# A graph attention layer on one core: f1's matmuls made 128 columns wide, x's sum moved to TensorE, the size test moved into later gaps, the last store split over two queues

## What is computed

```
x [4096, 128] f32, adj [4096, 4096] int32, W [128, 128], w1, w2 [1, 128], b1, b2 [1]
in_fts = W @ x.T
f1 = (w1 @ in_fts).T + b1          # one number per row
f2 = (w2 @ in_fts).T + b2          # one number per column
logits = f1 + f2.T
coefs = softmax(leaky_relu(logits) + where(adj > 0, 0, -1e9), axis=-1)
out = layernorm(x + coefs @ x, axis=-1)
```

## Time and profile before

| | |
|---|---|
| median of three runs | 273.05 us (272.51 to 273.35) |
| the profiled execution | 272.69 us, of which the profile's span is 270.8 us |
| busy in the span | PE 258.9, PEld 227.4, DVE 244.2, ACT 193.2, POOL 61.3 us |
| granted TensorE clock, mean | 0.994 |
| DMA | 73.64 MB, 272 GB/s over the span |

### The profile page before, as it was taken

How to read it: one execution, slowest core, us unless ns; L and a number is a source line. 1 busy time by engine, 2 the same in 40 slices (tenths; PEclk the granted TensorE clock), 3 DMA queues, 4 the chain that set the end, 5 groups by cost and what they waited for, 6 DMA issues and landing times.

```text
span 270.8 us, 5889 instructions
## 1 busy us (share of the span) xinstructions
PE 258.9 (96%) x2195; PEld 227.4 (84%) x2195; DVE 244.2 (90%) x310; ACT 193.2 (71%) x292; POOL 61.3 (23%) x87
## 2 busy tenths in 40 slices
PE   3989999999999999999999999999999999999990
PEld 3988988888888888888888888888888888888880
DVE  3899999999978999999999499999999999999963
ACT  2599899899999958992899329991999097104140
POOL 4022155000000051005940060006400600054150
PEclk9999999999999999999999999999999999999997
DMA  6999999999999999999999999999999999702011
GB/s 201 263 307 310 310 309 310 290 300 319 315 317 320 313 320 319 319 319 324 313 283 322 348 310 310 312 313 312 306 371 333 329 257 318 190 0 74 4 45 36
DMA packets 22258, 73.64 MB, mean 272 GB/s; under 512 B 2786, under 2 KB 3940, under 8 KB 22244
## 3 DMA queue, kind: packets, MB, share of 16 engines
q1 hardware_dynamic: 11104, 35.20, 43.0%
q10 hardware_dynamic: 9860, 34.61, 42.2%
q0 software_dynamic: 1280, 3.67, 4.6%
HBM read 71.37 MB, written 2.10 MB: 271 GB/s over the span
## 4 chain that ended last, share of the span: by engine, by line
DVE 48%; DMA 15%; PE 15%; issue 8%; ACT 7%; POOL 5%; ACTq 1%; DVEq 1%; POOLq 0%
DVE mn L737 16%; DVE msk L750 9%; DVE mn L742 9%; DMA nat<-in_adj 8%; PE ps L1094 8%; DMA out<-ybt 6%; ACT sgn L470 4%; PE ps L1051 3%; DVE post L858 3%; DVE ybt L873 3%; DVE bns L878 2%; PE ps L1038 2%; POOL xn L369 2%; DVE post L860 2%; DVE ntot L863 2%
## 5 line engine op out<-in xcount | busy, mean ns | idle before, releaser
L1094 PE MATMUL ps<-bt,msk 128*128 128x258 f16 x2048 | 230.3, 274 | 0.0
L1094 PEld LDWEIGHTS ps<-bt,msk 128*128 128x128 fp8e5 x2048 | 200.4, 98 | 29.4
L470 ACT ACTIVATE sgn<-f2b,nf1l 128x1024 int8<-128x1024 f32 x128 | 136.6, 1144 | 2.4 <-issue 1.6
L737 DVE TENSOR_SCALAR mn<-nat 128x4096 int8<-128x4096 int32 x32 | 73.2, 2287 | 3.0 <-DMA nat<-in_adj 2.7
L409 POOL TENSOR_SCALAR nmr<-mv 128x4 f32<-128x4 f32 x7 | 12.9, 1837 | 165.4 <-DVE mv L882 165.4
L615 ACT ACTIVATE ybt<-ybt,nmr,rstd 128x128 f32<-128x128 f32 x28 | 11.5, 483 | 44.1 <-POOL nmr L414 44.1
L750 DVE STREAM_TRANSPOSE msk<-mn 128x1024 uint32<-128x1024 uint32 x32 | 39.8, 1245 | 2.6
L742 DVE SCALAR_TENSOR_TENSOR mn<-sgn,mn 128x1024 uint32<-128x1024 uint32 x32 | 39.2, 1225 | 1.1
L608 ACT ACTIVATE post<-ps,ac 128x258 f32<-128x258 f32 x60 | 24.9, 468 | 10.3 <-PE ps L1094 10.3
L755 DVE TENSOR_SCALAR msk<-msk 128x1024 uint32<-128x1024 uint32 x32 | 22.2, 694 | 1.0
L1051 PEld LDWEIGHTS ps<-vsb,xn 128*128 128x128 f32 x64 | 14.2, 330 | 1.9 <-ACT xn L478 1.8
(11 more groups left out here) (112 smaller groups left out, 104.7 us busy)
## 6 DMA issues: line engine op xcount, KB each, us to landing
nat<-in_adj SPq DMA_DIRECT2D x64, 512.0 KB, 15.4
nat<-in_adj ACTq DMA_DIRECT2D x64, 512.0 KB, 18.5
xn<-in_x POOLq DMA_DIRECT2D x8, 256.0 KB, 12.1
out<-ybt POOLq DMA_DIRECT2D x12, 128.0 KB, 7.5
msk<-in_x SPq DMA_DIRECT2D x8, 128.0 KB, 4.1
msk<-in_x ACTq DMA_DIRECT2D x8, 128.0 KB, 4.4
out<-ybt SPq DMA_DIRECT2D x4, 64.0 KB
out<-post SPq DMA_DIRECT2D x4, 64.0 KB
```

Of the source, the lines that this page charges most:

```text
L470: ins = act.activation(sgn[:, c, g * JA:(g + 1) * JA], f2b[:, :], ACT.Sign, bias=nf1l[:, bass.ds(G * t + g, 1)], scale=-1.0)
L737: dve.tensor_scalar(mn[:, c % 2], nat[:, c], 0, EDGE, ALU.is_gt, ALU.mult).then_inc(cast_done, 1)
L1094: ins = pe.matmul(ps[:, 2 * c + m, 0:2 * DV], mask_f[c][m][:, n // KB, n % KB, :], btv[m][:, n, :], start=(n == first), stop=(n == last - 1))
```

## The change

1. f1_columns for groups 1 to 7 multiplies with the vector repeated 128 times, so each matmul streams 128 columns and writes 128 columns of ps, of which the next matmuls overwrite all but the first. Group 0 keeps its two columns (f1 and f2), with f2's now at column 300.
2. x's column sums are made on PE: 32 float32 matmuls with ones as weights (sum_x), in eight groups of four among the transposes and f1's. The accumulated sums in xT_out, their reduction on DVE and the matmul over xt1 go. xeps_out moves behind signs(2, 2) on ACT.
3. gram moves behind tile 0's minus matmuls, its last part behind tile 1's. The size test's steps move: gram's maximum behind turn(2, 2), stat_max(1, 2, 4) and stat_out(1, 2, 4) among the plus and low_x steps behind it; on PE turn_stats(1, 2, 4) into the middle of tile 2's minus matmuls and widen_stats(1, 2, 4) behind the first plus_sums of tiles 0 and 1.
4. Half of scale_x(0, 3) goes to ACT as scale_last, and the scale_x steps stand behind plus(2, 2).
5. POOL issues load_rows(1), the load of xn's second half, behind rows(0, 0) and no longer behind the next rows.
6. The last tile is stored in four pieces, two from SP and two from ACT, counted by end_stored, on which SP waits behind the end of the branch. SP's waits for the other stores move ahead of the wait for the last tile.

```
@@ block.sync, fast path
+                sp.wait_ge(out_stored, 16 * G * (NQ // 2 - 1))
+                sp.wait_ge(last_stored, 16 * (G + QT - 1))
                 sp.wait_ge(tile_ready, 1)
-                sp.dma_start(out_t[NT - 1], post[:, 1, 0, QT - 1, 0:D]).then_inc(last_stored, 16)
-                sp.wait_ge(out_stored, 16 * G * (NQ // 2 - 1))
-                sp.wait_ge(last_stored, 16 * (G + QT))
+                for g in range(G // 2):
+                    store_end(sp, g)
...
-            sp.nop()
+            sp.wait_ge(end_stored, 16 * G)
@@ block.gpsimd, fast path
                 rows(0, 0)
+                load_rows(1)
                 for turn in range(1, NQ // 2):
                     rows(2 * turn - 1, 1)
-                    if turn == 1:
-                        load_rows(1)
@@ block.scalar
-                act.activation(xT[:, b * 512:(b + 1) * 512], ps[:, 4 + b % 2, :], ACT.Copy,
-                               accum_out=xt8[:, b:b + 1]).then_inc(xT_ready, 1)
+                act.activation(xT[:, b * 512:(b + 1) * 512], ps[:, 4 + b % 2, :], ACT.Copy).then_inc(xT_ready, 1)
...
+            def scale_last():
+
+                act.wait_ge(cs_ready[0], 1)
+                act.wait_ge(table_ready[1], BCH)
+                for i in range(KB):
+                    n = (BCH - 1) * CN + i
+                    ins = act.activation(ybuf[:, BCH - 1, i], xl_chunk(BCH - 1)[:, i], ACT.Copy, scale=cs[:, 0, n:n + 1])
+                ins.then_inc(y3_act, 1)
...
             signs(2, 2)
+            xeps_out()
...
             load_far(QT + 2, 2)
+            scale_last()
             signs(3, 3, between={1: lambda: split_x(0, 2), 2: lambda: split_x(0, 3)})
...
                 normalise_last(1, 2, 1)
+                act.wait_ge(tile_ready, 1)
+                for g in range(G // 2, G):
+                    store_end(act, g)
@@ block.vector
             spread_f1(1, FIRST * KB, NK, 7, 0)
-            dve.wait_ge(xT_ready, NB)
-            dve.tensor_reduce(xt1[:, :], xt8[:, :], AX_X, ALU.add).then_inc(xt1_ready, 1)
...
-            dve.wait_ge(gram_made, 1)
-            dve.tensor_reduce(stat[:, 3:4], ps[:, 4, 0:D], AX_X, ALU.max).then_inc(stat_ready, 1)
             turn(1, 1)
 
             dve.wait_ge(cs_ready[0], 1)
             scale_x(0, 1)
-            stat_max(1, 2, 4)
             cast(2, 2, 0)
-            stat_out(1, 2, 4)
             combine(2, 2)
             dve.wait_ge(y_ready[0], 1)
             turn(2, 2)
+            dve.wait_ge(gram_made, 1)
+            dve.tensor_reduce(stat[:, 3:4], ps[:, 4, 0:D], AX_X, ALU.max).then_inc(stat_ready, 1)
 
             plus(0, 0)
             low_x(0, 1)
             plus(1, 1)
-            scale_x(0, 2)
+            stat_max(1, 2, 4)
             low_x(0, 0)
-            scale_x(0, 3)
+            stat_out(1, 2, 4)
             dve.wait_ge(y_act, 1)
             plus(2, 2)
+            scale_x(0, 2)
+
+            scale_x(0, 3, KB)
             low_x(0, 2)
             low_x(0, 3)
@@ block.tensor
-                        to, v = ps[:, bank, n - n0:n - n0 + 1], vsb[:, D:D + 1]
+
+                        to, v = ps[:, bank, n - n0:n - n0 + P], vsb[:, D:D + 1].to_broadcast([P, P])
...
+            def sum_x(b):
+
+                for n in range(b * KB, (b + 1) * KB):
+                    ins = pe.matmul(ps[:, 2, 0:D], ones[:, :], xl[:, n * D:(n + 1) * D], start=(n == 0), stop=(n == NK - 1))
+                if b == NB - 1:
+                    ins.then_inc(xsum_made, 1)
...
             turn_x(1)
+            sum_x(0)
...
+            sum_x(1)
             f1_columns(2)
             turn_x(4)
             turn_stats(0, 0, 2)
+            sum_x(2)
             f1_columns(3)
             turn_x(5)
+            sum_x(3)
             widen_stats(0, 0, 2)
             f1_columns(4)
             turn_x(6)
+            sum_x(4)
             f1_columns(5)
             turn_x(7)
+            sum_x(5)
+            sum_x(6)
             f1_columns(6)
+            sum_x(7)
             f1_columns(7)
...
-            gram(0)
-            gram(1)
+            pe.wait_ge(turn_done, 1)
+            pe.wait_ge(den_ready[1], 1)
+            minus_sums(0, 0)
+            minus_sums(0, 1)
...
+            minus_sums(0, 2)
+            minus_sums(0, 3)
+
+            pe.wait_ge(xT_ready, NB)
+            gram(0)
+            gram(1)
+            gram(2)
 
             pe.wait_ge(gst_ready, 1)
             pe.wait_ge(turn_done, 2)
             edge_sums(1, 1)
...
+            gram(3).then_inc(gram_made, 1)
             pe.wait_ge(turn_done, 3)
-            edge_sums(2, 1)
+            edge_sums(2, 1, 0, NK // 2)
+            turn_stats(1, 2, 4)
+            edge_sums(2, 1, NK // 2, NK)
...
             plus_sums(ORDER[0], range(2))
+            widen_stats(1, 2, 4)
             plus_sums(ORDER[1], range(2))
+
+            pe.wait_ge(stat_ready, 2)
```

More of the change, by code:

```diff
@@ L131, in gat_kernel @@
         ac = sb("ac", [P, 2, NT], F32)
-        xt8 = sb("xt8", [P, NB], F32)
-        xt1 = sb("xt1", [P, 1], F32)
         xeps = sb("xeps", [P, DV], F32)
@@ L155, in gat_kernel @@
         ORDER = (1, 0, 2, 3)
+        F2_AT = 300
         w_in = sem("w_in")
@@ L203, in gat_kernel @@
         y1_act = sem("y1_act")
+        y3_act = sem("y3_act")
         y_ready = [sem(f"y_ready{m}") for m in range(2)]
@@ L206, in gat_kernel @@
         table_ready = [sem(f"table_ready{m}") for m in range(2)]
-        xt1_ready = sem("xt1_ready")
         xsum_made = sem("xsum_made")
@@ L236, in gat_kernel @@
         out_stored = sem("out_stored")
+        end_stored = sem("end_stored")
         flag_ready = sem("flag_ready")
@@ L279, in load_part, with store_end @@
             eng.dma_start(dst, adj_v[t, a]).then_inc(nat_in[c], 16)
+        def store_end(eng, g):
+            eng.dma_start(out_t[NT - 1, g], post[g * SQ:(g + 1) * SQ, 1, 0, QT - 1, 0:D]).then_inc(end_stored, 16)
         @block.sync
@@ L335, in _ @@
                         apart(sp)
-            sp.nop()
+                sp.sem_inc(end_stored, 16 * G)
+            sp.wait_ge(end_stored, 16 * G)
         @block.gpsimd
@@ L477, in xT_out @@
                 act.wait_ge(x_turned, b + 1)
-                act.activation(xT[:, b * 512:(b + 1) * 512], ps[:, 4 + b % 2, :], ACT.Copy,
-                               accum_out=xt8[:, b:b + 1]).then_inc(xT_ready, 1)
+                act.activation(xT[:, b * 512:(b + 1) * 512], ps[:, 4 + b % 2, :], ACT.Copy).then_inc(xT_ready, 1)
             def f2_copy():
                 act.wait_ge(f1_made, 1)
-                act.activation(f2l[:, 0:KB], ps[:, 0, FIRST * KB:FIRST * KB + KB], ACT.Copy).then_inc(f2l_act, 1)
+                act.activation(f2l[:, 0:KB], ps[:, 0, F2_AT:F2_AT + KB], ACT.Copy).then_inc(f2l_act, 1)
             def f2_sums(i, n0):
@@ L525, in rows_out, with xeps_out @@
                 act.activation(nf1l[:, FIRST * KB:], ps[:, 6, 128 + FIRST * KB:256], ACT.Copy).then_inc(nf1l_ready, 1)
+            def xeps_out():
                 act.wait_ge(xsum_made, 1)
-                act.activation(xeps[:, 0:D], ps[:, 0, 0:D], ACT.Copy, scale=LOW * TINY / N).then_inc(xeps_ready, 1)
+                act.activation(xeps[:, 0:D], ps[:, 2, 0:D], ACT.Copy, scale=LOW * TINY / N).then_inc(xeps_ready, 1)
+            def scale_last():
[5 more added lines that the diff above has]
+                ins.then_inc(y3_act, 1)
             def split_x(m, h):
@@ L537, in split_x @@
                     act.wait_ge(y_ready[0], h)
+                    if h == BCH - 1:
+                        act.wait_ge(y3_act, 1)
                 act.activation(btv[m][:, h * CN:(h + 1) * CN, 0:D], ybuf[:, h], ACT.Copy,
@@ L1047, in f1_columns @@
                     if b == 0:
-                        to, v = ps[:, 0, n:n + FIRST * KB + 1:FIRST * KB], vsb[:, D:D + 2]
+                        to, v = ps[:, 0, n:n + F2_AT + 1:F2_AT], vsb[:, D:D + 2]
                     else:
-                        to, v = ps[:, bank, n - n0:n - n0 + 1], vsb[:, D:D + 1]
+                        to, v = ps[:, bank, n - n0:n - n0 + P], vsb[:, D:D + 1].to_broadcast([P, P])
                     ins = pe.matmul(to, xT[:, n * P:(n + 1) * P], v, start=True, stop=True)
@@ L1123, in _ @@
                       stop=True).then_inc(nf1_made, 1)
[L1124 to L1134, removed]
             minus_sums(0, 2)
             minus_sums(0, 3)
-            widen_stats(1, 2, 4)
+            pe.wait_ge(xT_ready, NB)
+            gram(0)
+            gram(1)
+            gram(2)
             pe.wait_ge(gst_ready, 1)
@@ L1141, in _ @@
             edge_sums(1, 1)
-            pe.wait_ge(xT_ready, NB)
+            gram(3).then_inc(gram_made, 1)
             pe.wait_ge(turn_done, 3)
-            edge_sums(2, 1)
+            edge_sums(2, 1, 0, NK // 2)
+            turn_stats(1, 2, 4)
+            edge_sums(2, 1, NK // 2, NK)
             pe.wait_ge(den_ready[0], 1)
```

## The result

The changed kernel takes 275.1 us, the median of nine runs (273.73 to 275.6), against 272.67 us for nine of the kernel before on the same chip (272.07 to 273.35). The ratio is 1.0074, 95% interval 1.0048 to 1.0101: slower by some 2.0 us by the ratio and 2.4 between the medians, where 3.9 were forecast. The profiled execution took 275.1 us with a span of 273.4, which is 2.4 and 2.6 us more than the one before.

What follows compares the result with a forecast made beforehand. PE's matmul stream was taken as the bound: tile 3 starting 3.8 us later plus 0.1 of tail, +3.9 on the profiled 272.69 us, made 276.6, 277.0 by the median; stated 276.9, range 273.4 to 283.0.

Steps and rivals of the forecast that it cites:

- The bound: PE's stream of 2048 matmuls at 0.1124 us each, never idle from 33.85 us, sets the time.
- The size test: Behind turn(2): copy to gst waits 1.8 us for PE, cast(3) follows after 12.1 us, not 8.6; alone +1.0 us.
- I take 18 us: PE's start: moment when TensorE's clock rises to 2.4 GHz, with bounds of 11 and 35 us.
- The forecast for a float32 matmul: sum_x on PE: 0.48 us per 128-column matmul at 1.2 GHz; four take 1.9 us, or 0.95 at 2.4 GHz.
- the two stalls: DVE waits for PE at its first spread_f1, 1.1 us, and at the first copy to gst, starting at 23.1 us.
- the list of signs: Closing list of what profiles would show, including DVE idle 1.1 us at first spread_f1 and 1.4 at first gst copy.
- early clock: Rival: clock up by about 14 us, first gst copy waits little, size test stays; 274.0 to 275.8 us, chance 0.18.
- the 2.8 us that I had put down to PE: DVE's delay at the first copy to gst, which starts at 23.1 us because it waits for PE's results.
- The lead that I named: DVE's lead over PE at tile 3, 1.6 us, as the most that anything done ahead of it can bring.
- The tail: Last tile's stores and final wait: bounds -0.7 and +0.5 us, taken as +0.1.
- Edits costed at nothing: Dropped accumulated sums on ACT, scale_last, moved xeps_out and the earlier load of xn's second half: no effect on time.
- The rule on transposes: Transposes don't count as busy for the clock, so it rises late; late-clock rival: 278 to 282 us, chance 0.24.

Runs made afterwards that it cites:

- e3: Kernel before with only f1's matmuls of groups 1 to 7 widened to 128 columns; 272.62 us, ratio 1.0005.
- e1: Changed kernel with only DVE's order behind turn(2, 2) altered: scale_x(0, 2) ahead of stat_max, half of scale_x(0, 3) and plus(2, 2) ahead of stat_out; 272.78 us, ratio 0.9986.
- e7: Kernel before with only the moved gram, the moved size test and scale_last; 276.3 us, ratio 1.0118.
- e8: Changed kernel with gram, the size test's steps, scale_x(0, 3) and xeps_out moved back to where they were; 272.27 us, ratio 0.9987.
- e6: Changed kernel with sum_x(0) moved from behind turn_x(1) to ahead of sum_x(1); 274.49 us, ratio 1.0066.
- e5: Kernel before with only the load of xn's second half, load_rows(1), moved forward; 273.56 us, ratio 1.0008.
- e9: Kernel before with e1's order, the new tail and the earlier rows, but narrow f1 and no sum_x; 272.82 us, ratio 1.0001.
- e2: Changed kernel with f1's matmuls back at one column, sum_x kept; 279.29 us, ratio 1.0143.
- e10: e1 with one more wait on SP: first adjacency loads issued only once x's third chunk has landed; 273.34 us, ratio 1.0013.

## Why the prediction was right in direction and twice too large

**The bound held.** The stream runs at 0.112 us a matmul in every kernel, and each profiled span but e3's follows from the start of minus(3) and the tail, within 0.2 us. The changed kernel: +3.2 - 0.6 = +2.6 us of span.

**The size test held, step by step.** Forecast: a wait of 1.8 us at the copy to gst, cast(3) 12.1 us behind turn(2), some 3 us of idle ACT, PE idle ahead of minus(3). Measured: 1.97, 12.3, 3.86, and waits of 0.79 and 1.46. e1, e7 and e8 show that this is the cause, and that nothing else in the change costs what the runs can tell.

**The step that failed is "I take 18 us".** The clock rose at about 10 us in the changed kernel (f1's 16 records take 2.05 us, were 3.58) and at 13 to 14 in e1, e3 and e6. The forecast for a float32 matmul was right at the low level (0.46 us against 0.48, in sum_x(0): 1.84 us from 7.57 to 9.41, four matmuls). So was 0.95 for four at the high level (0.89 between starts, 17.61 to 18.50), though the rows that I took "about half" from, 422 and 273 ns, say 0.65. So what was wrong was the level, and with it the two stalls. The first copy to gst starts at 21.90 without a wait, where I had 23.1 after one of 1.7 (23.1 - 21.4; the 1.4 in the list of signs doesn't fit these steps). f1_made is there at 11.9 us, so the wait of 1.1 at the first spread_f1 isn't there either. turn(2) ends at 42.3 instead of 43.4. This is the rival "early clock", whose 274.0 to 275.8 us hold the result; I gave it 0.18.

Yet turn(2) is 0.8 us later than before: DVE reached spread_f1 at 13.96 instead of 12.38, and made good 0.8 by the work that it lost (0.9 forecast). That delay is no stall on PE: DVE waits 0.86 and 0.88 us for x's chunks. I don't count it to the change. e5, whose start is untouched, shows the same waits (1.34 and 0.68 us), e8, with the changed start, has no late one. It varies between executions. So none of the 2.8 us that I had put down to PE was there in this execution, and x, late in it by chance, put DVE back by 1.6 us at spread_f1 and so filled part of the gap. That the number came as near as it did is luck to that extent.

**The lead that I named was not the tightest.** I took 1.6 us at tile 3 as the limit of any gain. At tile 2 it is 42.2 - 41.5 = 0.7 us, from the same rows. It explains why 1.9 us of earlier start (e3) and 2.4 (e8, 31.47 against 33.85) come out as 0.2 and 0.5: PE then waits for DVE at turn(2).

**The tail** is the second term that was mis-sized: +0.1 forecast, -0.6 measured, near the bound of -0.7. The +0.1 was picked between the bounds without a working; the four issues overlap on two queues (0.89 and 0.80 us, starting 0.06 apart). **Edits costed at nothing**: the moved load was worth nothing that is resolved (e5), and the wait at ybt for the store went, as said; scale_last and xeps_out had no run of their own.

**The sum with the measured terms**: the start of minus(2) +0.1, where 43.4 against 42.2 had been +1.2; from minus(2) to minus(3) +3.1, where it had been +2.6; the tail -0.6 instead of +0.1. Together that is +2.6 us of span instead of +3.9: 1.1 less from the clock, 0.7 less from the tail, 0.5 more behind turn(2).

**The rule on transposes.** From 5 us on, PE had transposes and narrow matmuls alone until 29.4 us in the kernel before and until about 30 in e7 and e9, and no rise before; in the changed kernel, e1, e2, e3, e6, e8 and e10 a group of ordinary 128-column matmuls stands ahead of every rise. That agrees with the Trainium skill, "TensorE: Matmul & The Clock Gate", Part 4, by which transpose mode does not count as busy in the same way. What I had drawn from it, a late rise, did not come: transposes between wide groups did no harm that a run shows, and they run at the high level themselves once it is there (eight in 1.03 us from 11.76 on, 1.97 from 5.81 on). No run had transposes alone, so whether they count is open. Open too is why the clock rose at 10 us in one execution and at 13.4 or later in another with the same start of the program (the changed kernel, e1).

## What to carry to other kernels

When a step that waits for another engine is moved, write down what stands behind it on its own engine: here two scale_x behind a 2 us wait, with a third engine's work hanging on them, cost 2.3 us, and putting them ahead of the wait gave that back. Count the bounding engine's lead at each early hand-over, not at one; the smallest is all that a faster start can bring. And look at what a clock gain would move before sizing it: PE finished its early work sooner, and stood still until DVE had turned the tile.

## What the runs showed of the hardware

- The clock can stay low while PE is booked busy. In e2 it goes from 1.00 through 0.83 to 0.50 between 12 and 16 us, with PE busy for 0.63 of 2.00 us from 12 to 14, and then stays at 0.50 through windows with 4.00 of 4.00 us busy, narrow f1 among them; with f1 wide, and 0.80 of 2.00 us busy at the same place, it stays at 1.00.
- 128 columns cost f1's matmuls little: eight records take 1.06 to 1.16 us wide and 0.95 narrow at 2.4 GHz (narrow in e2, 33.32 us), 2.08 wide (e3, 20.04 us) and 1.71 to 1.87 narrow at 1.2 GHz.
- The granted clock reads 1.00 from the start on, also where durations show the low level (sum_x(0) at 0.46 us a matmul, later 0.22 to 0.26). In these traces it is at odds with the durations only ahead of its first fall.
- The same load of x lands at least 1.5 us later in one execution than in another, with the same issues: DVE's fourth product starts at 11.25 us without a wait in the kernel before, and at 12.80 after a wait of 0.68 us in e5.
